# Two routed expert layers: gathers issued before the stores, one list copy per tile on GpSimd, and the result copied out before the weight pieces move

## The reference, cut to what matters

```python
x = x + conv0(ln_c(x))            # gating by row and column sums, group norms, softmaxes
t = tokens(x);  t = t + experts0(ln_t(t))     # 8 experts, hidden 512, silu(h) * g, top 2 of 8
x = x + conv1(ln_c(x))            # a 256x256 channel mix and a bias
t = tokens(x);  t = t + experts1(ln_t(t))     # 8 experts, hidden 1024, silu(h + b1), + b2, top 2 of 8
```

## Time and profile before

| | us |
|---|---|
| three runs: median (lowest, highest) | 1337.18 (1332.98, 1341.03) |
| the profiled execution's own time | 1330.54 |
| its span, first to last instruction | 1328.7 |
| PE busy (share of the span) | 954.9 (72%) |
| DVE busy | 806.6 (61%) |
| ACT busy | 595.0 (45%) |
| POOL busy | 509.3 (38%) |
| expert stage of layer 0 (first L712 to last L734) | 369.5 to 717.1 |
| expert stage of layer 1 (first L712 to last L734) | 905.4 to 1291.1 |

### The profile page before, as it was taken

How to read it: one execution, slowest core, us unless ns; L and a number is a source line. 1 busy time by engine, 2 the same in 40 slices (tenths; PEclk the granted TensorE clock), 3 DMA queues, 4 the chain that set the end, 5 groups by cost and what they waited for, 6 DMA issues and landing times.

```text
span 1328.7 us, 28374 instructions
## 1 busy us (share of the span) xinstructions
PE 954.9 (72%) x7185; PEld 790.8 (60%) x7185; DVE 806.6 (61%) x1970; ACT 595.0 (45%) x1332; POOL 509.3 (38%) x479
## 2 busy tenths in 40 slices
PE   5210375637688888888885388457999899999984
PEld 4100264624667666676774277426888787888873
DVE  6999488779755455455553676683455455555550
ACT  5265422228655555555553023283444344444442
POOL 1285000000036555666564140003555555556550
PEclk8655596555899999999998695558999999999996
DMA  7066204961857888888887704304555554554448
GB/s 254 1 198 209 75 0 118 337 186 48 269 125 183 182 180 174 186 194 192 192 182 182 257 0 153 109 1 95 120 104 117 127 122 85 135 134 75 77 74 264
DMA packets 210851, 189.97 MB, mean 143 GB/s; under 512 B 98992, under 2 KB 184440, under 8 KB 210680
## 3 DMA queue, kind: packets, MB, share of 16 engines
q1 hardware_dynamic: 150632, 108.48, 28.5%
q0 software_dynamic: 27440, 38.97, 18.3%
q10 hardware_dynamic: 32736, 42.02, 9.8%
HBM read 111.22 MB, written 58.79 MB: 128 GB/s over the span
## 4 chain that ended last, share of the span: by engine, by line
PE 34%; DMA 22%; issue 17%; DVE 11%; ACT 6%; ACTq 3%; POOL 2%; DVEq 1%; SPq 1%; POOLq 1%
PE bank L734 12%; PE bank L712 12%; DMA wreg<-in_L_ffn_w_dram 7%; DMA region<-rows_x,fetch_now 5%; DMA rows_y<-region,put_now 5%; PE bank L645 4%; DMA xt<-region 3%; PE bank L562 2%; PE bank L617 1%; POOL rows_y L498 1%; ACT wreg L830 1%; PE bank L770 1%; DVE region L1066 1%; PE bank L687 1%; DVE region L1418 1%
## 5 line engine op out<-in xcount | busy, mean ns | idle before, releaser
L712 PE MATMUL bank<-xt,wreg 128*128 x3360 | 391.0, 278 | 59.3 <-DMA xt<-region 52.1
L712 PEld LDWEIGHTS bank<-xt,wreg 128*128 128x128 f16 x3360 | 331.1, 100 | 113.5 <-issue 69.1
L498 POOL DMA_INDIRECT rows_y<-region,put_now x140 | 240.0, 1714 | 189.5 <-ACT region L953 87.7
L734 PE MATMUL bank<-wreg,region 128*128 128x256 f16 x2520 | 291.5, 274 | 24.0 <-DVE region L1413 13.9
L734 PEld LDWEIGHTS bank<-wreg,region 128*128 128x128 f16 x2520 | 242.4, 98 | 64.8 <-DVE region L1413 16.4
L458 POOL DMA_INDIRECT region<-rows_x,fetch_now x144 | 145.9, 1013 | 158.7 <-issue 82.6
L936 ACT ACTIVATE region<-bank,b_t,wreg 128x256 f32<-128x256 f32 x280 | 135.6, 562 | 20.6 <-issue 12.2
L953 ACT ACTIVATE region<-region 128x256 f32<-128x256 f32 x70 | 31.7, 500 | 207.3 <-DVE region L1418 202.0
L1410 DVE TENSOR_SCALAR region<-region,wreg 128x512 f16<-128x512 f32 x140 | 71.0, 507 | 65.6 <-ACT region L936 57.6
L1413 DVE SCALAR_TENSOR_TENSOR region<-region,wreg 128x512 f16<-128x512 f32 x140 | 105.2, 752 | 5.0
L562 PE MATMUL bank<-ident,xn 128*128 128x128 f32 x256 | 54.4, 372 | 58.9 <-DVE xn L1037 52.8
(11 more groups left out here) (241 smaller groups left out, 1312.5 us busy)
## 6 DMA issues: line engine op xcount, KB each, us to landing
wreg<-in_L_ffn_w_dram SPq DMA_DIRECT2D x48, 512.0 KB, 6.8
wreg<-in_L_ffn_w_dram ACTq DMA_DIRECT2D x72, 256.0 KB
split_v<-wreg ACTq DMA_DIRECT2D x36, 512.0 KB
wreg<-in_L_ffn_w_dram SPq DMA_DIRECT2D x64, 256.0 KB, 3.0
wreg<-split_v SPq DMA_DIRECT2D x32, 512.0 KB
rows_x<-region SPq DMA_DIRECT2D x16, 512.0 KB, 4.5
rows_y<-tok SPq DMA_DIRECT2D x16, 512.0 KB, 4.9
tok<-rows_y SPq DMA_DIRECT2D x16, 512.0 KB, 6.0
```

The lines of the kernel that those rows point to most:

```text
L498: nc.gpsimd.indirect_dma_start(rows_y[f], bass.IndirectOffsetOnAxis(ap=put_now[:, g_:g_ + 1], axis=0), y_rows[:, g_, :], None, compute_op= ...
L712: last = pe.matmul(to, block, x_cols[:, bass.ds(b, 1), :, xs_, k, :].rearrange("p j r n -> p (j r) n"), start=(k == 0 and ws_ + xs_ == 0), ...
L734: last = pe.matmul(yb[:, r * C:(r + 1) * C], lhs[:, c, r * P:(r + 1) * P], block, start=first, stop=end, skip_group_check=True)
```

## The change

- **POOL**: one copy per tile of four numbers, the gather rows of tile t + 3 and the store rows of tile t. One `after` loop then waits for the copy, for both transposes of tile t + 1 and for the weights of tile t + 1. The gathers of tile t + 3 are issued, then one `after` loop waits for `y_copied`, and the stores of tile t are issued. So the gather of tile t + 3 now stands before the store of tile t, not behind it. There is no wait for `y_free` on POOL inside the loop. Three tiles are gathered before the loop from the list `first_rows`, without a copy.
- **ACT, layer 0**: L946 and its waits stand ahead of `move_pieces`.
- **DVE**: `pick_weights(n + 1)` stands at the start of tile n, and the wait for `y_free` is gone in layer 0; the weights have four buffers.
- The lists are shifted by six columns in place of two, and the small tiles move inside `region`.

```diff
-                def put(n, copied):
-                    pool.wait_ge(y_free[f], 32 * n + 16)
-                    nc.gpsimd.tensor_copy(put_now[:], moves[:, bass.ds(2 * n, 2), 1]).then_inc(puts_copied[f], 1)
-                    after(n, lambda m: pool.wait_ge(puts_copied[f], m + 1))
-                    after(copied, lambda m: pool.wait_ge(y_copied[f], m))
...
-                fetch_next(0, 1)
-                fetch_next(1, 0)
+                def first_fetch(n):
+                    for r in range(2):
+                        free(pool, xr_loaded[r][f], 16 * n)
+                        free(pool, xc_ready[r][f], 16 * (n - 1))
+                        free(pool, weights_ready[f], n - 1)
+                        fetch(f, n % 2, r, first_rows[:, 2 * n + r:2 * n + r + 1])
...
                 with pool.Fori(0, total // 2) as p:
                     for b in range(2):
-                        put(2 * p + b, 2 * p + b + 1)
-                        fetch_next(2 * p + b + 2, 1 - b)
+                        t = 2 * p + b
+                        for r in range(2):
+                            pool.wait_ge(xr_loaded[r][f], 16 * t + 48)
+                        copy_lists(t, b)
+                        def may_fetch(m):
+                            pool.wait_ge(lists_copied[f], m + 1)
+                            for r in range(2):
+                                pool.wait_ge(xc_ready[r][f], 16 * m + 32)
+                            pool.wait_ge(weights_ready[f], m + 2)
+                        after(t, may_fetch)
+                        for r in range(2):
+                            fetch(f, 1 - b, r, now[:, b, r, 0:1])
+                        after(t, lambda m: pool.wait_ge(y_copied[f], m + 1))
+                        put(b)
@@ ACT, experts, f == 0
                             split_hi(n)
-                            move_pieces(n)
                             act.wait_ge(y_ready[f], n + 1)
                             act.wait_ge(y_free[f], 32 * n + 16)
                             act.wait_ge(factors_y_ready, n + 1)
...
                             last.then_inc(y_copied[f], 1)
+                            move_pieces(n)
@@ DVE, experts
                     with dve.Fori(edges[e], edges[e + 1]) as n:
+                        pick_weights(f, n + 1)
...
-                        else:
-                            dve.wait_ge(y_free[f], 32 * n + 16)
-                        pick_weights(f, n + 1)
                         if f == 0:
                             split_lo(n)
@@ DVE, lists
-                chain(dve.tensor_scalar(moves[:, 0:GROUPS - 2, 0], moves[:, 2:GROUPS, 1], NT * P - 1, None, ALU.bitwise_and))
+                chain(dve.tensor_scalar(moves[:, 0:GROUPS - 6, 0], moves[:, 6:GROUPS, 1], NT * P - 1, None, ALU.bitwise_and))
```

More of the change, by code:

```diff
@@ L101, in bass_metaformer @@
         weighed = region[:, 7864:7872].rearrange("p (j g k) -> p j g k", j=2, g=2)
-        weights = region[:, 7872:7876].rearrange("p (j g) -> p j g", j=2)
-        factors_y = region[:, 7876:7880].rearrange("p (j g) -> p j g", j=2)
+        weights = region[:, 7872:7880].rearrange("p (j g) -> p j g", j=4)
+        factors_y = region[:, 7880:7884].rearrange("p (j g) -> p j g", j=2)
         g = wreg[:, 0:8192].rearrange("p (k n) -> p k n", k=KC)
@@ L188, in bass_metaformer @@
         bias_rows = routed
-        fetch_now, put_now = sb("fetch_now", [P, 2], U32), sb("put_now", [P, 2], U32)
-        first_rows = sb("first_rows", [P, 2], U32)
+        now = region[:, 7888:7896].bitcast(U32).rearrange("p (b g m) -> p b g m", b=2, g=2)
+        first_rows = region[:, 7896:7902].bitcast(U32)
         count16 = sb("count16", [P, P], F16)
@@ L259, in bass_metaformer @@
         listed, list_taken = sem("listed"), sem("list_taken")
-        fetches_copied, puts_copied = two("fetches_copied"), two("puts_copied")
+        lists_copied = two("lists_copied")
         ids_listed = sem("ids_listed")
@@ L483, in feed_experts @@
                 pool.wait_ge(weights_kept[f], 17)
-                for r in range(2):
-                    fetch(f, 0, r, first_rows[:, r:r + 1])
+                def first_fetch(n):
[4 more added lines that the diff above has]
+                        fetch(f, n % 2, r, first_rows[:, 2 * n + r:2 * n + r + 1])
+                first_fetch(0)
@@ L497, in put, with copy_lists @@
+                def copy_lists(t, b):
+                    nc.gpsimd.tensor_copy(now[:, b], moves[:, bass.ds(2 * t, 2), :]).then_inc(lists_copied[f], 1)
+                def put(b):
                     for g_ in range(2):
-                        nc.gpsimd.indirect_dma_start(rows_y[f], bass.IndirectOffsetOnAxis(ap=put_now[:, g_:g_ + 1], axis=0),
+                        nc.gpsimd.indirect_dma_start(rows_y[f], bass.IndirectOffsetOnAxis(ap=now[:, b, g_, 1:2], axis=0),
                                                      y_rows[:, g_, :], None, compute_op=ALU.add).then_inc(y_free[f], 16)
-                def fetch_next(n, b):
-                    for r in range(2):
-                        pool.wait_ge(xr_loaded[r][f], 16 * n + 16)
-                    nc.gpsimd.tensor_copy(fetch_now[:], moves[:, bass.ds(2 * n, 2), 0]).then_inc(fetches_copied[f], 1)
-                    after(n, lambda m: pool.wait_ge(fetches_copied[f], m + 1))
-                    for r in range(2):
-                        if isinstance(n, int):
-                            free(pool, xc_ready[r][f], 16 * n)
-                            free(pool, weights_ready[f], n)
-                        else:
-                            after(n, lambda m: pool.wait_ge(xc_ready[r][f], 16 * m))
-                            after(n, lambda m: pool.wait_ge(weights_ready[f], m))
-                        fetch(f, b, r, fetch_now[:, r:r + 1])
@@ L526, in all_done, with may_put @@
+                        put(b)
+                last = total // 2 * 2
+                copy_lists(last, 0)
+                def may_put(m):
+                    pool.wait_ge(lists_copied[f], m + 1)
+                    pool.wait_ge(y_free[f], 32 * m + 16)
+                after(last, may_put)
+                after(total, lambda m: pool.wait_ge(y_copied[f], m))
+                put(0)
                 def all_done(m):
@@ L953, in experts @@
                                 last = act.activation(y_rows[:, g_, :], y_rows[:, g_, :], ACT.Copy,
-                                                      scale=weights[:, bass.ds(n % 2, 1), g_:g_ + 1].rearrange("p a b -> p (a b)"))
+                                                      scale=weights[:, bass.ds(n % 4, 1), g_:g_ + 1].rearrange("p a b -> p (a b)"))
                             last.then_inc(y_copied[f], 1)
```

17 lines of the change are left out of this document (8 added, 9 removed).

## The result

| | before | after |
|---|---|---|
| median of the runs side by side (lowest, highest) | 1339.11 (1332.98, 1342.13) | 1296.26 (1294.19, 1301.47) |
| profiled execution, its span | 1330.54, 1328.7 | 1295.54, 1293.7 |
| layer 0: distance of tile starts | 9.94 | 9.22 |
| layer 1: first up to last up | 375.1 | 363.2 |

The ratio is 0.9692, 95% interval 0.9645 to 0.9738: 42.9 us faster.

What follows compares the result with a forecast made beforehand. The weight pieces' ring was to bound layer 0 at 9.6 us per tile instead of 9.94: 11.6 saved, plus 2.5 and 1.5 at the last tile, 15.6; 1337.2 - 15.6 = 1321.6 us, own range 1313 to 1333, wide 1292 to 1345.

Steps and rivals of the forecast that it cites:

- Ring of gathers: Layer 0: the ring grows from three tiles to four, asks 7.1 us per tile; PE's 37.8 us row waits lose their cause.
- The last is the one that the change makes longer: Layer 0's weight pieces: split, y's copy, store and loads to the next split, 2.37 + W, 9.6 us per tile.
- W: Layer 0: time from a weight piece's store issue to the next split; taken as 7.2 us, between 3.2 and 8.53.
- ACT in series 8.5: Layer 0: ACT's silus, splits, y's copy and issue of piece transfers, one after another, need 8.5 us per tile.
- rival A: Layer 0: pieces come in time, ACT, `y_rows` or transfer engines rule at 8.5 to 8.7 per tile; 1288 us, chance 0.17.
- ring of the pieces: Layer 0: the next split needs loads issued by move_pieces, now behind y's copy; forecast to set 9.6 us per tile.
- POOL 7.3: POOL's own work per tile, waiting for nothing, falls from 8.96 to 7.3 us, or 7.8 if waits cost and not loops.
- `pick_weights` at 0: DVE, layer 0: picking weights early gains 0; the 76.9 us wait for `y_free` was idle time off the path.
- Last tile: Layer 0's end: 2.5 us won by the earlier y copy and store, 1.5 by a faster last up.
- The change leaves both as they are: 0: Layer 1: PE's 13.9 us of waits and the 33.2 us for late-landing stores beside weight loads stay; gain 0.
- Rival B: Layer 0: no change, W is 7.6 and the pieces' ring 10.0 per tile; 1336 us, chance 0.25.
- Rival C: Layer 0: stores land late beside piece transfers and hold up y's copy, 10.5 per tile; slower, 1355 us, chance 0.15.

Runs made afterwards that it cites:

- e2: The after kernel with POOL issuing the stores of tile t before the gathers of tile t + 3, as before: 1318.7 us.
- e5: The before kernel with ACT's part of the change alone, y's copy ahead of the pieces' transfers in layer 0: 1345.26 us, ratio 1.0026 to before.
- e1: The after kernel with the pieces' transfers on ACT in layer 0 ahead of the copy of y again: 1287.3 us.
- e10: e1 with layer 0's gathers in the loop cut to 8 bytes per row, into a place nothing reads: 1281.07 us.
- e12: The after kernel with one more ACT copy per tile of layer 0, right behind the split and ahead of the transfer issues: 1298.12 us.
- e13: The after kernel with one more ACT copy per tile of layer 0, behind move_pieces and ahead of the next silu: 1301.14 us.
- e14: The after kernel with the two loads of the next weight piece issued by SP in place of ACT: 1279.33 us.
- e3: The after kernel with the old two copies and seven one-round loops per tile on POOL, gathers still ahead of stores: 1307.15 us.
- e4: The after kernel with pick_weights(n + 1) at the end of tile n again, in layer 0 behind the wait for y_free: 1366.95 us.
- e9: The after kernel with layer 1's weight loads issued by SP only when DVE has finished the next tile's first low part: 1312.37 us.
- e6: The after kernel with SP in layer 1 waiting for the landing of the last tile's store before issuing weight loads: 1301.47 us.
- e7: The after kernel with SP in layer 1 issuing weight loads only after POOL's copy behind the last tile's store: 1297.7 us.

## Why the prediction was wrong, step by step

**Ring of gathers: right.** PE's wait for rows fell from 37.8 us to nothing that the waits show, where "below 8" was forecast. The granted clock of the stage rose from 0.96 to 0.99.

**"The last is the one that the change makes longer", W = 7.2: wrong in its size. This is the step that failed in layer 0.** In after, W has a minimum of 6.05 and a median of 6.3, and in the four tiles where the trace has the load end the wait 6.4 to 7.5. The part in front of it, from the split to the store, is 2.7 (median) and not 2.37. The ring is 9.0, not 9.6, and the tile 9.22.

The 7.2 was wrong in two ways. It was read in a tile where the split did not wait, and there the distance says when ACT came, not when the load landed. The semaphore events of the two loads tell it: the last one that the trace records for a piece came 6.2 us after the store's issue in before (median; 4.7 to 7.9) and 5.5 in after (5.2 to 6.9). And the row belonged to a kernel with its gathers behind the stores, which the change itself removes. With that order the forecast's ring is there: in e2, which differs from after in POOL's order alone, the split waits for its piece in 23 tiles (W 7.3, tile 9.70), in e5 in 23 (W 7.1, tile 10.07). e1 shows W of 7.0 to 7.8 once the pieces go out earlier, and e10 that it is the gathers that hold them up then.

The ring is not far off in after either. In 12 of 34 tiles the split starts 0.62 to 0.64 after its piece's last event, the shortest distance that occurs, so the piece came just in time there; most of the rest lie within 0.9. The prediction's estimate of 4.4 for W was made for GpSimd's path, while the pieces are ACT's transfers; no piece in after landed in under 5.2.

**"ACT in series 8.5": mis-sized.** This is rival A's mechanism, which had 0.17. From the silu to the split it is 3.96 (median; 3.91 computed), from the split to the next silu 4.98, where the prediction added 1.33 + 0.1 + 0.84 + 2.33 = 4.60. The 2.33 was the idle time in front of L946 in a kernel where the first issue came 1.43 after the split's start (627.65 to 629.08), prepared while the split executed. With y's copy ahead it comes 2.2 to 3.5 after it (median 2.7; 2.88 in the tile shown, 566.48 to 569.36), and nothing covers the rest. 3.96 + 4.98 = 8.9 of the 9.22. The ring of the pieces is as long: 8.3 from the split to the last landing and 0.6 to the next split. e12 and e13 lengthen ACT's series too little to tell, and e14 shortens both rings. So which of the two sets the 9.22 is not shown. The gain is 34 x (9.94 - 9.22) = 24.6 us in place of 11.6.

**"POOL 7.3": too low, without effect.** In e14's profile, where POOL hardly waits, it is 8.3 from gather to gather (565.43 to 573.74). The gap in front of the stores is 0.75 where the sum had 0.30, the gap in front of the gathers 1.26 for 1.00, the two stores 3.78 for 3.52. It binds at once when the old copy and loops are back (e3): they are worth 11 us, so "neither sets the end" holds for the new order alone.

**`pick_weights` at 0: right as a cost,** but e4 shows it as a condition for the rest, which the prediction's "off the path" hid.

**Last tile: nearly right.** 3.2 us from the last up to the token load, forecast 2.5 + 1.5 = 4.0.

**"The change leaves both as they are: 0" in layer 1: the second step that failed.** It was 11.9 us, half as much as layer 0 gave. The prediction looked at POOL, DVE and ACT, and saw the late landings beside weight loads, but not why the load stood there: SP issues it in order behind transposes that wait for a gather, and the gather was moved. Before, the load was issued between 1.6 us ahead of the second store and 1.3 behind it, in all six; after, 4.8 ahead. e9 restores the coincidence alone and loses 16 us, e2 restores most of it by POOL's order and loses 9.5 in layer 1. The "same 10.5 us per tile" of the forecast's signs was misread too: it is 375.1 / 34 = 11.0 before and 10.7 after.

**Start of layer 1**: 2.5 us lost, inside the bounds of -2 to +3.

Rival A's 1288 is nearer to 1296.26 than the forecast, but by luck: its 49.6 us were all of layer 0 and the stage's end, which gave 27.8, and it had nothing for layer 1. Rival B, no change by a longer W, is e5's case in time, and its ring is there in 23 tiles. Rival C did not come: ACT's copy of y waited for the store's landing in 2 tiles, 1.5 us.

What each part is worth, by undoing it alone: the gathers' place 22 us in both layers (e2), with the early weights as its condition (e4); the fewer copies and loops 11 (e3); the place of layer 1's load 16 (e9). ACT's part cost 9 (e1), and brought nothing by itself (e5). These overlap and do not add up. Left open: which of two rings sets the 9.22 of after, and what sets e14 at 8.77 exactly, with PE at 0.96, the transfer engines at 0.90, POOL at 8.3 and the split waiting for its loads again, 20.3 us in 16 tiles.

## What to carry to other kernels

When an instruction moves, follow every engine that waits for it, also the one that only issues transfers: what is queued behind its wait moves too, and here that was a 2 MB load. A wait measured in the kernel before holds for the placement before; where the change moves the transfers it competes with, take it as a bound and not as the value. On an engine that issues transfers and executes, add up the issue where nothing executes beside it, and test the bound by taking issue away, not by adding execution; then look whether that moved another ring as well. A distance up to an instruction that did not wait is a bound from above on what it could have waited for, and not its time.

## What the runs showed of the hardware

- The second of a tile's two indirect stores (128 rows) landed 9.99 us after its issue when a 2 MB load was issued 0.5 us later (1042.98 to 1052.97). By the place of the load, over the six loads of a run: 1.6 us ahead to 1.3 behind 6.8 to 10.0 (before), 0.6 ahead 8.4 to 9.6 (e9), 1.4 to 3.0 ahead 6.8 to 9.2 (e2), 4.8 ahead 5.2 to 7.2 (after), 5.2 to 6.7 ahead 4.8 to 7.1 (e6), 2.3 to 3.0 behind 3.9 to 4.6 (e7). PE lost 13.9, 15.7, 11.0, 3.5, 1.9 and 1.9 us in these stages. So a load up to 6.7 us ahead still delayed the store; what it cost PE fell to a few us from 4.8 ahead on.
- An operation of 0.6 us on ACT behind three transfer issues (e13) lengthened the stretch from the split to the next silu from 5.01 to 5.31 us, where runs with the same code as after read 5.01 to 5.13. In front of the issues (e12) it was 5.14.
- 512 KB stored and 2 x 256 KB loaded on ACT's queue had their last landing 5.5 us after the store's issue (after, median) and 6.3 when only POOL's gathers stood behind its stores (e2).
- The same 512 KB of loads per tile issued by SP and not by ACT took 17 us off the median (1296.26 to 1279.33).
- The trace puts a silu's late start down to PE's bank (61.9 us in 24 waits) when in the tile shown the silu came 4.66 us after the start of up, and in before as early as 1.54; only that distance told it.
